# Exponent bounds on ScalarE instead of mask products on TensorE, and work moved at the phase boundaries, in a hybrid of two state-space mixers and an FFN

## What is computed

```python
# mixer a: 16 heads x 64, state 64
gate, hBC, dt = split(x @ in_proj_w.T)
hBC = silu(causal_conv(hBC, 4 taps) + conv_b)
h, Bm, Cm = split(hBC)
dt = softplus(dt + dt_bias); A = -exp(A_log)
A_cs = cumsum(A * dt)                           # within a chunk
L = exp(segment_sum(A * dt))                    # -inf above the diagonal
Y_diag = einsum(Cm, Bm, L, h * dt)
Y_off = Cm @ state * exp(A_cs)                  # state carried over chunks
y = Y_diag + Y_off + D * h
yf = y * silu(gate)
out = (norm_w * yf * rsqrt(mean(yf * yf) + EPS)) @ out_proj_w.T
# mixer b: 64 heads x 16, state 128; the same recurrence, written step by step:
state = state * exp(dt * A) + (dt * x) outer B;   y = C @ state + D * x
out = (y * rsqrt(mean(y * y) + EPS) * norm_w * silu(z)) @ out_proj_w
# ffn, 4 steps on the last token of each sequence
thought = layer_norm(x)[:, -1] @ agg_w + agg_b
for _ in range(4):
    t = gelu(layer_norm(thought) @ d1_w + d1_b)
    thought = thought + t @ d2_w + d2_b
out = layer_norm(x + sigmoid(x @ gate_w + gate_b) * (thought @ bc_w + bc_b))
# the whole
x = x + mixer_a(norm(x)); x = x + ffn(norm(x))
x = x + mixer_b(norm(x)); x = x + ffn(norm(x))
```

## Time and profile before

| | us |
|---|---|
| median of 3 runs | 2988.8 |
| lowest and highest | 2985.39, 2990.64 |
| profiled execution, its own time | 2990.27 |
| its span | 2988.6 |
| mean granted TensorE clock | 0.972 |

### The profile page before, as it was taken

How to read it: one execution, slowest core, us unless ns; L and a number is a source line. 1 busy time by engine, 2 the same in 40 slices (tenths; PEclk the granted TensorE clock), 3 DMA queues, 4 the chain that set the end, 5 groups by cost and what they waited for, 6 DMA issues and landing times. The chain is left out here.

```text
span 2988.6 us, 54351 instructions
## 1 busy us (share of the span) xinstructions
PE 2784.4 (93%) x19824; PEld 1846.6 (62%) x19824; DVE 2020.4 (68%) x3697; ACT 1249.0 (42%) x2098; POOL 955.8 (32%) x618
## 2 busy tenths in 40 slices
PE   6999999999999997995899999999999999997996
PEld 5677666666666764454666666666666666663443
DVE  4666666666566663377777777787777777775268
ACT  3344444334443431341454444544545444453242
POOL 2232223322233231242333333233333333323144
PEclk9999999999999997997999999999999999998898
DMA  4000000010000033144000000000000000013233
GB/s 127 15 29 21 21 21 21 21 34 22 21 21 24 19 113 141 43 155 181 11 23 22 21 21 14 21 21 21 14 14 21 21 21 21 11 62 133 93 108 132
DMA packets 80673, 140.16 MB, mean 47 GB/s; under 512 B 18120, under 2 KB 18632, under 8 KB 79568
## 3 DMA queue, kind: packets, MB, share of 16 engines
q1 hardware_dynamic: 70448, 126.44, 12.3%
q10 hardware_dynamic: 10144, 12.64, 1.4%
HBM read 104.98 MB, written 33.55 MB: 46 GB/s over the span
## 5 line engine op out<-in xcount | busy, mean ns | idle before, releaser
L613 PE MATMUL work<-b_xnT,shared_w 128*128 128x256 f32 x2304 | 548.6, 389 | 6.2 <-DVE b_parts L1125 6.1
L613 PE MATMUL work<-a_xnT,shared_w 128*128 128x256 f32 x2176 | 501.6, 386 | 6.1 <-DVE a_parts L1125 4.8
L613 PEld LDWEIGHTS work<-b_xnT,shared_w 128*128 128x128 f32 x2304 | 425.4, 191 | 89.4 <-issue 20.0
L613 PEld LDWEIGHTS work<-a_xnT,shared_w 128*128 128x128 f32 x2176 | 409.4, 192 | 78.2 <-issue 18.3
L1165 DVE TENSOR_TENSOR b_decay<-b_decay,b_gt 128x1024 f32<-128x1024 f32 x256 | 354.2, 1420 | 28.5 <-ACT b_decay L889 24.5
L889 ACT ACTIVATE b_decay<-seg 128x1024 f32<-128x1024 f32 x256 | 251.4, 1021 | 174.8 <-PE seg L739 174.0
L1375 POOL TENSOR_TENSOR a_y<-a_y,a_skip 128x1024 f32<-128x1024 f32 x32 | 103.4, 3231 | 513.8 <-DVE a_y L1154 513.8
L1340 POOL TENSOR_TENSOR b_rhs<-b_l_side,of_head 128x1024 fp32r<-128x1024 f32 x32 | 82.0, 2562 | 579.1 <-DVE b_l_side L1134 579.1
L841 ACT COPY shared_z<-work 128x256 f32<-128x256 f32 (+1 forms) x192 | 84.8, 442 | 414.3 <-PE work L613 414.3
L1044 DVE SCALAR_TENSOR_TENSOR shared_cv<-shared_pre,b_conv_w,shared_cv 128x256 f32<-128x256 f32 x480 | 222.4, 492 | 46.4 <-ACT shared_cv L835 38.6
L720 PE MATMUL work<-b_w_out,b_yz 128*128 128x512 f32 x512 | 226.8, 596 | 8.2 <-DVE b_y L1154 8.2
(11 more groups left out here) (314 smaller groups left out, 4523.6 us busy)
## 6 DMA issues: line engine op xcount, KB each, us to landing
shared_x<-in_L_attn_a_x SPq DMA_DIRECT2D x16, 512.0 KB, 3.7
a_x_res<-in_L_attn_a_x SPq DMA_DIRECT2D x32, 256.0 KB, 2.7
x_mid<-a_x_res SPq DMA_DIRECT2D x32, 256.0 KB, 2.0
shared_w<-in_L_ffn_d_w SPq DMA_DIRECT2D x2, 4096.0 KB, 12.9
f_d_w<-in_L_ffn_d_w SPq DMA_DIRECT2D x2, 4096.0 KB, 15.0
f_x_res<-x_mid SPq DMA_DIRECT2D x8, 1024.0 KB, 6.2
f_bc_w<-x_mid SPq DMA_DIRECT2D x8, 1024.0 KB, 5.6
shared_x<-x_mid SPq DMA_DIRECT2D x16, 512.0 KB, 3.6
```

Of the source, the lines that this page charges most:

```text
L613: mm = nc.tensor.matmul(dst, w_in[:, k, col:col + m], xnT[:, k, :], start=(k == 0), stop=(k == KD - 1))
```

## The change

It does five things. (1) The mask products are gone, with their constants and transfers. (2) Instead ScalarE makes two passes: `slot_bound` takes Relu of the negated exponent out of PSUM into `decay` and raises `seg_taken`, for which the next unit of TensorE now waits, and `slot_exp` takes Exp of the negated result in place. Exponents below the diagonal are not positive, so they come out as before, and positive ones become 0 and their Exp 1, where `gt` is zero. Both slots of a unit are bounded first; in the first half a step of `fill0` goes between the two Exps. (3) In mixer B, `z2` moves from slot 7 to slot 5; `z1` stays at 3. (4) norm_w is loaded by SyncE inside the mixer stage under a semaphore of its own; small1's sums go ahead of the scaling of w_out in the first supertile; the FFN transposes two tiles, then does the last rows, then the other two; its last store goes in two halves, B's x is loaded at group 4, and GpSimd waits for `done` before add_beta. (5) `keep_running` runs products of the identity with itself: 12 at the start of a mixer, 10 at its end, 24 at the start of an FFN, 14 at the end of the first FFN.

```diff
+def keep_running(nc, bank, ident, count):
+    for _ in range(count):
+        nc.tensor.matmul(bank[:, 0:P], ident[:], ident[:], start=True, stop=True)
...
+def load_norm(eng, dst, w, loaded):
     eng.dma_start(dst["norm_w"][:], w["norm_w"].rearrange("(k p) -> p k", p=P)).then_inc(loaded, 16)
...
+        if NP > 2:
+            fill1 = [[], [], [], ["z1"], [], ["z2"]] + [[]] * (NS - 6)
...
                 load_x(1)
                 load_res(0, 0)
+                with nc.allow_non_contiguous_dma(reason="small vectors"):
+                    load_norm(sp, c["vectors"][cfg.tag], w, c["norm_loaded"][cfg.tag])
                 if later:
-                    for b in range(4):
-                        for q in range(4):
-                            sp.dma_start(c["masks"][32 * q:32 * q + 32, b], c["masked_bf"][32 * b:32 * b + 32]
-                                         ).then_inc(c["masks_loaded"], 16)
                     with nc.allow_non_contiguous_dma(reason="small vectors"):
                         load_ffn_vectors(sp, c["ffn"], c["ffn_w"], c["ffn_loaded"])
...
-                    pe.wait_ge(exp_done, FREE + tile * NS + 2 * p)
+                    pe.wait_ge(seg_taken, FREE + tile * NS + 2 * p)
                     for k in range(4):
                         slot, half, r = unit_bank(p, k)
-                        nc.tensor.matmul(seg[k // 2][:, (k % 2) * 512:(k % 2 + 1) * 512], lhs[r:r + 32, p // 2, :],
-                                         rhs[p // 2][r:r + 32, 4 * half:4 * half + 4, :].rearrange("p h l -> p (h l)"),
-                                         start=True, stop=True)
-                    for b in range(3, -1, -1):
-                        for k in range(4):
-                            r, n = unit_bank(p, k)[2], 32 * (b + 1)
-                            out = seg[k // 2][32 * b:32 * b + 32, (k % 2) * 512:(k % 2 + 1) * 512]
-                            mm = nc.tensor.matmul(out.rearrange("p (h l) -> p h l", h=4)[:, :, 0:n],
-                                                  c["ident_bf"][r:r + 32, r:r + 32], c["masks"][r:r + 32, b, :, 0:n],
-                                                  start=False, stop=True, skip_group_check=True)
-                            if b == 0 and k % 2 == 1:
-                                mm.then_inc(seg_full, 1)
+                        mm = nc.tensor.matmul(seg[k // 2][:, (k % 2) * 512:(k % 2 + 1) * 512], lhs[r:r + 32, p // 2, :],
+                                              rhs[p // 2][r:r + 32, 4 * half:4 * half + 4, :].rearrange("p h l -> p (h l)"),
+                                              start=True, stop=True)
+                        if k % 2 == 1:
+                            mm.then_inc(seg_full, 1)
...
+                keep_running(nc, seg[0], ident, 12)
                 run(prologue(), pro_steps[:2])
...
                 run(epilogue(), epi_steps)
+                pe.wait_ge(exp_done, FREE + 2 * NSUP * NS)
+                keep_running(nc, seg[0], ident, 10)
...
-                def slot_exp(sec, j, s):
+                def slot_bound(sec, j, s):
                     tile = 2 * sec.i + j
                     act.wait_ge(seg_full, tile * NS + s + 1)
                     act.wait_ge(ydiag_done, FREE + 2 + tile * NS + s - 3)
                     nc.scalar.activation(decay[:, slot_buffer(j, s)].rearrange("p h l -> p (h l)"),
-                                         seg[s % 2][:, :], ACT.Exp).then_inc(exp_done, 1)
+                                         seg[s % 2][:, :], ACT.Relu, scale=-1.0).then_inc(seg_taken, 1)
+                def slot_exp(sec, j, s):
+                    tile = 2 * sec.i + j
+                    act.wait_ge(seg_taken, FREE + tile * NS + s + 1)
+                    d = decay[:, slot_buffer(j, s)].rearrange("p h l -> p (h l)")
+                    nc.scalar.activation(d, d, ACT.Exp, scale=-1.0).then_inc(exp_done, 1)
...
                     gate_silu(i)
+                    slot_bound(sec, 0, 0)
+                    slot_bound(sec, 0, 1)
                     slot_exp(sec, 0, 0)
                     if prev:
...
                     for p in range(NP):
+                        behind = fill0[2 * p + 1] if nxt else []
                         if nxt:
                             fills(sec, fill0[2 * p])
                         if p + 1 < NP:
+                            slot_bound(sec, 0, 2 * p + 2)
+                            slot_bound(sec, 0, 2 * p + 3)
                             slot_exp(sec, 0, 2 * p + 2)
+                            fills(sec, behind[:1])
                             slot_exp(sec, 0, 2 * p + 3)
-                        if nxt:
-                            fills(sec, fill0[2 * p + 1])
+                            fills(sec, behind[1:])
+                        else:
+                            fills(sec, behind)
                     square(2 * i)
                     if nxt:
                         z_copy(sec, "z0a")
+                    slot_bound(sec, 1, 0)
+                    slot_bound(sec, 1, 1)
                     slot_exp(sec, 1, 0)
                     if nxt:
                         z_copy(sec, "z0b")
...
                             fills(sec, fill1[2 * p])
                         if p + 1 < NP:
+                            slot_bound(sec, 1, 2 * p + 2)
+                            slot_bound(sec, 1, 2 * p + 3)
                             slot_exp(sec, 1, 2 * p + 2)
                             slot_exp(sec, 1, 2 * p + 3)
...
                     dve.wait_ge(out_loaded, 16)
+                    dve.wait_ge(c["norm_loaded"][cfg.tag], 16)
...
                         out_add(sec, "pout", i - 1, 1)
-                    else:
+                    small_sums(sec, 1)
+                    if not prev:
                         norm_into_w_out()
-                    small_sums(sec, 1)
...
-                dve.wait_ge(small_loaded, 16 * 6)
+                dve.wait_ge(small_loaded, 16 * 5)
...
                 def store(n):
+                    if n == GROUPS - 1:
+                        for h in range(2):
+                            sp.wait_ge(done, NT * n + 2 * (h + 1))
+                            sp.dma_start(dst_t[n][:, 2 * h:2 * h + 2], x_res[n % 2][:, 2 * h:2 * h + 2]
+                                         ).then_inc(stored[n % 2], 16)
+                        return
...
-                    load_z(sp, to_w, mw, signals("z_loaded"))
+                    return lambda: load_z(sp, to_w, mw, signals("z_loaded"))
 
                 for n in range(GROUPS):
                     store(n)
                     if n + 2 < GROUPS:
                         load_res(n + 2)
+                    if n == 4 and following:
+                        load_rest = load_next_phase()
                     if n == 5 and following:
-                        load_next_phase()
-                for s in stored:
-                    sp.wait_ge(s, 16 * (GROUPS // 2))
+                        load_rest()
+                for k, s in enumerate(stored):
+                    sp.wait_ge(s, 16 * (GROUPS // 2) + 16 * k)
...
-                for t in range(NT):
-                    prepare(0, t)
+                keep_running(nc, seg[1], ident, 24)
+                prepare(0, 0)
+                prepare(0, 1)
                 pe.wait_ge(rows_ready, 1)
                 for k in range(KD):
                     mm = nc.tensor.matmul(col_ps[:, k * BATCH:(k + 1) * BATCH], last[:, k * P:(k + 1) * P],
                                           ident[0:BATCH, 0:BATCH], start=True, stop=True)
                 mm.then_inc(lastT_full, 1)
+                prepare(0, 2)
+                prepare(0, 3)
...
+                if following:
+                    pe.wait_ge(done, NT * GROUPS)
+                    keep_running(nc, work[0], ident, 14)
...
                     if n >= 1 and n + 1 < GROUPS:
+                        pool.wait_ge(done, NT * (n + 1))
                         add_beta(n + 1)
```

30 lines of the change are left out of this document (9 added, 21 removed).

## The result

| | us |
|---|---|
| kernel before, median of 11 runs | 2986.47 (2983.41 to 2990.64) |
| changed kernel, median of 11 runs | 2978.02 (2976.05 to 2984.61) |
| ratio, 95% interval | 0.9972 (0.9963 to 0.9980) |
| span of the profiled run, before and after | 2988.6, 2977.0 |

What follows compares the result with a forecast made beforehand. TensorE's own instruction stream was taken as the bound. Loops +10.2, start -8.5, small_sums -2, FFN starts -13, FFN to B -3.9, B's start -3.8, end -3.5: -24.5 from 2988.8 gives 2964 us, range 2932 to 2993.

Steps and rivals of the forecast that it cites:

- the masks (-52.3): Both mixer loops: dropping the mask products frees TensorE 0.327 us in each of 160 units, -52.3 us.
- The cost of a pass (0.93): ScalarE in the mixers: a 128x1024 pass in a row of others costs 0.93 us, from PSUM or SBUF.
- rival C: Mixers: an Exp in place costs more than 0.93 us; at 0.3 us lost per pair, 3000 us; chance 0.12.
- The wait of yoff1a in A and B: Mixers' second half: yoff1a waits for the copy of z0b, 1.65 us in A, 0.96 in B, 15 supertiles each.
- The wait of small1 (+15.8): Mixer A, first half: small1 waits 1.05 us for VectorE's out_add, in 15 supertiles.
- rival A: Mixer loops: the added passes are hidden after all, the 62.5 us of waits go, 2909 us; chance 0.12.
- only place (2) is wrong: Mixer A, first half: only the forecast wait of small1 behind out_add is missing, 2948 us; most of a 0.12 chance.
- The last supertile of B: Mixer B's end, no blocks to hide under: ScalarE's four passes (3.7 us) set the pace per pair, +7.5 us.
- The start: Kernel start: without norm_w on ScalarE's queue the barrier falls at about 8.7 and block 1 comes earlier, -8.5 us.
- The FFN starts: Both FFN starts: identity products lift the clock and reordered last rows bring the serial chain forward, -6.5 us each.
- rival B: Seams: the identity products do not lift the clock and only occupy TensorE, 2984 us; chance 0.12.
- FFN to B, B's start, the end: Seam into mixer B -3.9 us, B starting at full clock -3.8, second FFN's finish and split last store -3.5.

Runs made afterwards that it cites:

- e2: The changed kernel with ScalarE's copy of z0b moved between the two Relu passes of the second half, in both mixers: 2927.0 us.
- e1: The changed kernel with the load of w_out moved behind the landing of mixer A's small vectors: 2976.8 us.
- e5: The kernel of e2 with w_out loaded late as in e1: 2921.9 us.
- e9: e2 with VectorE waiting for three early vectors before dt and the two convolution vectors behind it, and mixer A's w_out loaded behind these two: 2919.2 us.
- e6: e2 without any of the identity products (no call of keep_running): 2931.2 us.
- e10: e9 with 28 identity products instead of 24 at the FFN start and 5 more behind the first two transposed tiles: 2915.0 us.
- e8: e2 without GpSimd's new wait on done before add_beta: 2931.0 us.

## Why the prediction was right or wrong

- **What bounds the kernel, and the masks (-52.3).** Right. B's period fell by 2.49 us in e2, eight times 0.33 less 0.15 that no row names, which also bounds what the move of z2 costs; A's by 0.49, two times 0.33 less small1's 0.16. That TensorE's busy time would be lower by some 50 us was wrong, since the identity products put 29.4 back.
- **The cost of a pass (0.93).** Right. ScalarE in the last supertile of B:

```profile
2717.32 2.00 ACT L895 ACTIVATE b_decay<-b_decay 128x1024 f32<-128x1024 f32 x2
2719.21 1.94 ACT L888 ACTIVATE b_decay<-seg 128x1024 f32<-128x1024 f32 x2
2721.02 2.02 ACT L895 ACTIVATE b_decay<-b_decay 128x1024 f32<-128x1024 f32 x2
```

  From start to start a pair of Exps in place takes 1.89 us and a pair of Relus out of PSUM 1.81, so rival C, the in-place Exp that costs more, is refuted. (The Trainium skill, "ScalarE: Activation LUTs", in the section that times the ACTIVATE, leads to an estimate of 0.95 us back to back; the trace agrees with 0.94 for the Exp, and has 0.91 for the Relu.)
- **The wait of yoff1a in A and B.** Right: 1.54 and 0.74 us against 1.65 and 0.96, and e2 shows that nothing else of the passes costs more than 0.2 us a period in the loops. (The working took the 0.33 us by which a unit comes earlier off the copy's start in B and not in A; with it A's wait would have been put at 1.3.) That the wait could be avoided for nothing by moving the copy up I had not seen.
- **The wait of small1 (+15.8).** Wrong step: that VectorE's multiplication keeps its 2.18 us when it moves. It fell to 1.32, and small1 waited 0.16 us where 1.05 had been put, 13 us less over the 15 periods. The dips of the clock, which no step of the sum had, cost 14. That A's term came out within 0.2 us is luck. Of rival A ("only place (2) is wrong", 2948) the missing wait came true and the time did not. (That rival takes "the 62.5 us of waits" away and reckons with 55: the 7.5 of B's last supertile stay in its 2909.)
- **The last supertile of B.** The pace is right: the rows above have 3.7 us from pair to pair, where it was 3.05. That the stretch came out at +3.5 against +4.9 shows less, since its granted clock is 0.91 where it was 0.98, which the term did not have.
- **The start (-8.5, measured +1.1).** This is the step that failed, and most of the 13 us between forecast and profile. The barrier moved as worked out. But I kept conv_b's landing at 15.6 us after its issue, a number that the trace had measured with the queues' load as it was before, while the same step let 2 MB start beside it: it landed after 24.0. e1 and e5 bring the landing back to 17.9 and 17.7, and with it the first Silu by 4.8 us and 5, half of the miss. The other half is a landing 2 us later than 15.6 even so, and a copy of block 1 at 28.3 in e1 where 24 to 26 had been worked out. e9 takes the wait off the path: its first Silu is at 47.9, 10.3 us ahead of the kernel before.
- **The FFN starts (-6.5 each, measured -4.2 and -3.0).** The mechanism was half right. The reorder brings the serial chain forward, and by e6 all of the gain is its. The lift of the clock came in part, 0.77 over the first 30 us where 0.51 had been and 1.00 was forecast, so rival B's sign (it stays at 0.51) did not show. The step that failed is the time put on it: e6, at 0.66 without the products, is as fast. B's start, where the clock rises to 1.00, gained as forecast. e10 shows what was in the way, since 1.2 and 1.1 us of idling followed the products: with these filled the clock is 0.89 over the first FFN's first 30 us and the start 2.5 us shorter. (The Trainium skill, "TensorE: Matmul & The Clock Gate", Part 4 on the transpose mode, has transposes not counted as busy. That agrees with the fall of the clock behind the first transposes here, but in e10 the clock stays up through transposes of the same number once the waits beside them are filled, so these runs don't separate the transposes from the idling.)
- **FFN to B, B's start, the end.** Right within 0.4 us each; e8 puts add_beta's wait at some 4 us over both FFNs, of which its profile shows 2.5 behind the first stores, and e6 the identity products at the seam at 3.4 us less 1.8.
- **The chances.** The forecast had a 0.12 for rival B, whose time (2984) was nearer to the result than the forecast's. What came was no rival as written: the forecast's mechanisms, with the start wrong and the FFN starts worth half.

## What to carry to other kernels

A landing time in a trace belongs to the load on the queues at that moment: when a change lets a large transfer start earlier, every small transfer that is still under way can become later, and whoever waits for it must be costed anew. When an engine with room to spare gets more work, look for the copies behind it that free a bank, and put them ahead of the new work; here that one exchange was worth 51 us, six times the whole change. On TensorE count a new wait with what follows it: a wait of 1.5 us was followed by half clock that cost up to 1.7 us in 8 of its 15 places.
